# Graph attention with residual and layer norm: the left term worked out per four groups, context kept whole on chip, x loaded before the first strips

## The chip, the core and the metric

The kernel runs on one core of a Trainium2 chip. Its time is the device time of one execution in microseconds, given as the median of several runs. The engines are TensorE (PE; its weight loads are listed apart as PEld), VectorE (DVE), ScalarE (ACT), GpSimd (POOL) and SyncE (SP), which here issues every DMA.

## What is computed

N is 8192 rows, x is [8192, 256], context is [8192, 512], adj is an 8192 x 8192 matrix of zeros and ones in float32 (268 MB). Cut to what matters:

```python
in_fts = context @ W_common.T                 # 512 -> 256
left  = in_fts @ w_left + b_left              # one number per row
right = in_fts @ w_right + b_right            # one number per column
logits = left[:, None] + right[None, :]
logits = where(logits >= 0, logits, 0.2 * logits)
logits = where(adj <= 0, -inf, logits)
out = layernorm(x + relu(softmax(logits) @ x))
```

Neither term needs the 256-wide product: `context @ (W.T @ w)` is one dot product of 512 elements per row and side.

## The kernel before

**Layout.** The columns of adj are split into four quadrants of 2048 (`Q`, `NQ`), one per 32 partitions. A strip is 32 rows of adj (`B`), laid out as 128 partitions x 2048, 1 MB, and there are 256 of them (`NS`). Four strips make a group of 128 output rows (`SG`), and there are 64 groups (`NG`). The strips rotate through four buffers (`NB`); the transposed weights `T` have two halves, used by even and odd groups.

**Main part, per strip n.** SP loads it with four DMAs (`load_strip`, L172 to L176) once the buffer is free, that is after `transposed(n - 4)`. ACT turns it into a mask (`keep`, L351). DVE combines it with the column table `tab` (in PSUM) and the row's own word `arow[:, n]` (`masked`, L518, a maximum and a minimum), and transposes it in 32 x 32 blocks into `T` (`transposed`, L562). DVE's order is `masked(n + 1)`, `transposed(n)`; the first transpose of a group waits until PE has finished the group before last. Each float32 word holds a high and a low float16, and `X` holds x scaled, as a high and a low float16 too. PE makes a group's product from 64 x 3 matmuls: high with high (L291), low with high (L292), high with low (L295), each 128 x 257. Then follow the division, the residual, the mean, the variance and the normalisation, shared between DVE, ACT and POOL (L567, L332, L572, L336, L340, L255 to L259, L345), and a store.

**Setup.** SP loads W, two weight vectors and two biases, then the context in eight chunks of 2 MB (`NCH`, L200) through four places in `X`, then strips 0 and 1, then, after the left sums, strips 2 and 3, then x in four chunks (L212). Half of x (`xs1`) lies in `T[:, 1]`, the half of T that group 1 uses. DVE makes all 64 right dots and 24 of the left ones (`OWN`, L418), POOL multiplies for the 40 other left ones (L249), and ACT sums them (L305). Then one chain of small operations (L426 to L482) makes the exponentials, `tab` and all 256 columns of `arow`. ACT squares x in 64 steps to find its scale (L321), DVE makes the factors `Fx` (L489 to L504), ACT writes the 64 high parts of x (L326) and DVE the 64 low parts (L510). DVE has the first four strips transposed before the scale is known (they share no data with it), and it holds back `masked(4)` until the low parts are made. PE's group 0 waits for the high and low part of every block j in turn. SP issues nothing between the last x chunk and the end of the low parts (L214, L215); only then come two rows of x for the residual and strip 4:

```python
sp.wait_ge(s_xh, JB)
sp.wait_ge(s_xl, JB)
for g in range(2):
    load_xrow(g)
```

There is also a general path (`Else`) for data of a wide spread; it isn't taken with these inputs.

Of the kernel before, what the change touches and what calls it, by code (L numbers as in the profile page):

```python
# [11 lines left out]
AX = mybir.AxisListType  # L12

# [9 lines left out]
def build(nc, x, adj, ctx_in, w_common, w_left, b_left, w_right, b_right, out):  # L23
# [3 lines left out]
    P = 128  # L27
# [12 lines left out]
    NX = 4  # L40
    XC = JB // NX
    HB = JB // 2
    OWN = [j for j in range(JB) if j % 8 in (0, 3, 6)]
# [13 lines left out]
    with stack:  # L57
# [14 lines left out]
        LR = sb("LR", [P, 2, JB])  # L72
        E = sb("E", [P, 2, JB])
        Et = sb("Et", [P, 2, JB])
        word = sb("word", [P, 2, JB])
        gen = sb("gen", [P, 2, JB])
        F = sb("F", [P, JB])
        Fx = sb("Fx", [P, JB])
        SS = sb("SS", [P, JB])
        wcol = sb("wcol", [P, 2, HID // P])  # L80
        bias = sb("bias", [P, 2])
        small = sb("small", [P, 64])
        y = xs2[:, 0:NY, :]
        xrow = xs2[:, NY:NY + 2, :]

# [4 lines left out]
        word16 = word[:, :, :].rearrange("p c j -> p (c j)").bitcast(F16).rearrange("p (c j e) -> p c j e", c=2, e=2)  # L90
        cstage = [Xflat[:, s * CT * CIN:(s + 1) * CT * CIN].rearrange("p (t k) -> p t k", k=CIN) for s in range(4)]
        xs1 = T[:, 1, :, :].rearrange("p j m -> p (j m)").rearrange("p (j d) -> p j d", d=D)
        W = strip[:, 3, 0:2 * CIN].rearrange("p (h k) -> p h k", h=2)
        wrep = strip[:, 3, 2 * CIN:2 * CIN + 4 * P].rearrange("p (c h m) -> p c h m", c=2, h=2)
        vl = strip[:, 2, 0:CIN]
        prod = strip[:, 2, CIN:3 * CIN].rearrange("p (b k) -> p b k", b=2)

        def xrows(j):
            return xs1[:, j, :] if j < HB else xs2[:, j - HB, :]
# [10 lines left out]
        mxc, diag = small[0:3, 28:29], small[0:3, 29:32]  # L110

# [4 lines left out]
        pt = stack.enter_context(nc.psum_tensor("pt", [P, 512], F32))  # L116
        tab = stack.enter_context(nc.psum_tensor("tab", [P, NQ], F32))
# [5 lines left out]
        s_ctx = [sem(f"context_in{s}") for s in range(4)]  # L123
# [3 lines left out]
        s_vl = sem("v_left_copied")  # L127
        s_prod = sem("product_ready")
        s_sum = sem("product_summed")
        s_dot = sem("dots_done")  # L130
        s_lr = sem("left_right_ready")
# [14 lines left out]
        s_xl = sem("x_low_ready")  # L146
        s_one_col = sem("ones_column_steps")
# [23 lines left out]
        def _(sp):  # L171
# [14 lines left out]

            sp.dma_start(W, w_common.rearrange("(p h) k -> p h k", p=P)).then_inc(s_w, 16)
            for c, v in enumerate((w_right, w_left)):
                sp.dma_start(wcol[:, c, :], v.rearrange("(p h) -> p h", p=P)).then_inc(s_w, 16)
            for c, v in enumerate((b_right, b_left)):  # L190
                sp.dma_start(bias[:, c:c + 1], v.broadcast_to([P, 1])).then_inc(s_w, 16)
            for c in range(NCH):
                if c >= 4:
                    end = (c - 3) * CT
                    own = sum(j < end for j in OWN)
                    sp.wait_ge(s_dot, end + own)
                    sp.wait_ge(s_prod, end - own)
                for q in (0, 2, 1, 3):
                    rows = ctx_in[q * NQ + c * CT * B:q * NQ + (c + 1) * CT * B, :]
                    sp.dma_start(cstage[c % 4][q * B:(q + 1) * B, :, :],  # L200
                                 rows.rearrange("(t p) k -> p t k", p=B)).then_inc(s_ctx[c % 4], 16)
            for n in range(2):
                load_strip(n)
            sp.wait_ge(s_sum, JB - len(OWN))
            sp.wait_ge(s_v, 1)
            for n in range(2, NB):
                load_strip(n)
            for c in range(NX):
                dst = (xs1, xs2)[c // (NX // 2)][:, c % (NX // 2) * XC:(c % (NX // 2) + 1) * XC, :]
                for q in (0, 2, 1, 3):  # L210
                    r0 = q * NQ + c * XC * B
                    sp.dma_start(dst[q * B:(q + 1) * B, :, :],  # L212
                                 x[r0:r0 + XC * B, :].rearrange("(j p) d -> p j d", p=B)).then_inc(s_x[c], 16)
# [427 lines left out]
```

## Time and profile before

| | us |
|---|---|
| median of 3 runs | 1564.39 |
| lowest, highest | 1547.11, 1564.72 |
| profiled execution | 1557.17 |
| its span, first to last instruction | 1555.3 |

| engine | busy us | share |
|---|---|---|
| PE | 1379.9 | 89% |
| PEld | 1199.8 | 77% |
| DVE | 1269.4 | 82% |
| ACT | 685.9 | 44% |
| POOL | 110.2 | 7% |

The busy shares are means over a setup of about 200 us and a main part of about 1350 us, with different limits. For the setup the rows to read are those of single engines in order of time. For the main part they are one group's period and what ended the idle time before each line.

### The profile page before, as it was taken

What the parts mean: (1) busy time and instruction counts of PE and PEld (TensorE: products, weight loads), DVE (VectorE), ACT (ScalarE), POOL (GpSimd) and SP (SyncE); (2) the same over time, 40 slices, a digit from 0 to 9 for tenths busy, and PEclk for the clock granted to TensorE, in tenths of its full rate; (3) what the DMA queues carried; (4) which work ended last, traced back from release to release, by engine and by line L of the source; (5) the groups of instructions that cost most, each with busy time, mean ns of one, the idle gap of its engine ahead of it and who ended that gap; (6) DMA issues with size and microseconds to landing.
All of it is one profiled execution on the core that took longest, in us unless ns stands there. A gap on an engine that the chain in (4) does not pass through costs nothing.

```text
span 1555.3 us, 28279 instructions
## 1 busy us (share of the span) xinstructions
PE 1379.9 (89%) x12302; PEld 1199.8 (77%) x12302; DVE 1269.4 (82%) x1000; ACT 685.9 (44%) x852; POOL 110.2 (7%) x240
## 2 busy tenths in 40 slices
PE   1002379999999999999999999999999999999998
PEld 0002268888888888888888888888888888888887
DVE  4883698898888988888988888888889888889881
ACT  2458544444444444444444444444444444444440
POOL 4710000000000000000000000000000000000000
PEclk7555789999999999999999999999999999999999
DMA  9994598888888888888888888888888888888870
GB/s 212 270 200 87 139 220 208 221 206 207 211 208 216 213 205 211 206 207 224 203 210 210 208 210 220 205 207 211 209 218 211 205 212 208 207 223 204 208 177 12
DMA packets 85584, 312.82 MB, mean 201 GB/s; under 512 B 19792, under 2 KB 44368, under 8 KB 52688
## 3 DMA queue, kind: packets, MB, share of 16 engines
q1 hardware_dynamic: 85456, 310.98, 81.2%
q8 instruction: 96, 1.57, 0.5%
q14 instruction: 32, 0.26, 0.1%
HBM read 302.52 MB, written 8.39 MB: 200 GB/s over the span
## 4 chain that ended last, share of the span: by engine, by line
PE 87%; DMA 5%; SPq 4%; DVE 3%; ACT 1%; POOL 0%; issue 0%; POOLq 0%; DVEq 0%
PE ps L295 29%; PE ps L291 29%; PE ps L292 29%; DMA X<-in_L_gnn_context_dram 3%; SPq L212 2%; DVE X L510 2%; DMA xs<-in_x_dram 1%; SPq L200 1%; DMA strip<-in_adj_dram 1%; ACT pt L321 1%; SPq L175 1%; DVE gw L418 0%; DVE strip L518 0%; DVE T L562 0%; POOL strip L249 0%
## 5 line engine op out<-in xcount | busy, mean ns | idle before, releaser
L291 PE MATMUL ps<-X,T 128*128 128x257 f16 x4096 | 1117.3, 273 | 34.5 <-DVE T L562 32.8
L295 PE MATMUL ps<-X,T 128*128 128x257 f16 x4096 | 1125.2, 275 | 0.0
L292 PE MATMUL ps<-X,T 128*128 128x257 f16 x4096 | 1114.8, 272 | 0.0
L562 DVE STREAM_TRANSPOSE T<-strip 128x2048 f32<-128x2048 f32 x256 | 589.4, 2303 | 174.8 <-PE ps L295 174.8
L351 ACT ACTIVATE strip<-strip 128x2048 f32<-128x2048 f32 x256 | 488.8, 1910 | 413.7 <-DMA strip<-in_adj_dram 413.4
L518 DVE SCALAR_TENSOR_TENSOR strip<-tab,arow,strip 128x2048 f32<-128x2048 f32 x256 | 595.1, 2325 | 17.3 <-ACT strip L351 17.0
L291 PEld LDWEIGHTS ps<-X,T 128*128 128x128 f16 x4096 | 403.5, 99 | 85.0 <-DVE T L562 33.0
L292 PEld LDWEIGHTS ps<-X,T 128*128 128x128 f16 x4096 | 399.0, 97 | 61.3
L295 PEld LDWEIGHTS ps<-X,T 128*128 128x128 f16 x4096 | 397.2, 97 | 63.2 <-DVE X L510 7.5
L332 ACT ACTIVATE xs<-ps,small 128x256 f32<-128x256 f32 x64 | 30.4, 475 | 219.9 <-DVE small L567 219.9
L255 POOL TENSOR_SCALAR small<-small 128x1 f32<-128x1 f32 x64 | 12.3, 192 | 1398.9 <-ACT pt L340 1398.9
L336 ACT ACTIVATE small<-small 128x1 f32<-128x1 f32 x64 | 13.0, 203 | 156.2 <-DVE xs L572 156.2
L418 DVE SCALAR_TENSOR_TENSOR gw<-X,ps 128x512 f32<-128x512 f32 x88 | 54.2, 683 | 20.7 <-DMA X<-in_L_gnn_context_dram 20.7
L273 PE MATMUL pt<-ident,small 128*2 128x128 f32 x1 | 0.4, 372 | 69.0 <-DVE small L433 69.0
L273 PEld LDWEIGHTS pt<-ident,small 128*2 128x2 f32 x1 | 0.1, 80 | 70.1 <-issue 70.1
L249 POOL TENSOR_TENSOR strip<-X,strip 128x512 f32<-128x512 f32 x40 | 49.6, 1273 | 32.5 <-DMA X<-in_L_gnn_context_dram 32.5
L277 PE MATMUL pt<-ident,small 128*1 128x128 f32 x1 | 0.4, 372 | 55.5 <-DVE small L489 55.5
L277 PEld LDWEIGHTS pt<-ident,small 128*1 128x1 f32 x1 | 0.1, 79 | 55.6 <-DVE small L489 55.6
L305 ACT ACTIVATE strip<-strip 128x512 f32<-128x512 f32 x40 | 25.2, 630 | 38.8 <-POOL strip L249 38.8
L345 ACT ACTIVATE xs<-xs,small 128x256 f32<-128x256 f32 x64 | 37.5, 586 | 3.6 <-POOL small L259 3.6
L257 POOL TENSOR_TENSOR small<-small 128x1 f32<-128x1 f32 x64 | 35.2, 551 | 5.3
L340 ACT ACTIVATE pt<-xs,small 128x256 f32<-128x256 f32 x64 | 30.6, 478 | 2.1
(71 smaller groups left out, 198.3 us busy)
## 6 DMA issues: line engine op xcount, KB each, us to landing
strip<-in_adj_dram SPq DMA_DIRECT2D x1024, 256.0 KB, 4.6
X<-in_L_gnn_context_dram SPq DMA_DIRECT2D x32, 512.0 KB, 16.9
xs<-in_x_dram SPq DMA_DIRECT2D x64, 128.0 KB, 5.0
out_dram<-xs SPq DMA_DIRECT2D x64, 128.0 KB, 4.9
T<-in_x_dram SPq DMA_DIRECT2D x8, 512.0 KB, 13.9
xs<-in_x_dram SPq DMA_DIRECT2D x8, 512.0 KB, 14.1
strip<-in_L_gnn_W_common_dram SPq DMA_DIRECT2D x1, 512.0 KB, 3.6
wcol<-in_L_gnn_w_right_dram SPq DMA_DIRECT2D x1, 1.0 KB, 3.3
```

What stands on the lines that cost most here:

```text
L212: sp.dma_start(dst[q * B:(q + 1) * B, :, :], x[r0:r0 + XC * B, :].rearrange("(j p) d -> p j d", p=B)).then_inc(s_x[c], 16)
L249: nc.gpsimd.tensor_tensor(prod[:, m % 2, :], cstage[c % 4][:, t, :], vl, ALU.mult).then_inc(s_prod, 1)
L257: nc.gpsimd.tensor_tensor(st(5, o), st(4, o), power, ALU.pow).then_inc(s_rstd, 1)
L291: nc.tensor.matmul(ps[o][:, 0:D + 1], hi, X16[:, jb, 0:D + 1], start=(jb == 0), stop=False)
L292: nc.tensor.matmul(ps[o][:, 0:D + 1], lo, X16[:, jb, 0:D + 1], start=False, stop=False)
L295: m = nc.tensor.matmul(ps[o][:, 0:D + 1], hi, X16[:, jb, D + 2:2 * D + 3], start=False, stop=(jb == JB - 1))
L345: nc.scalar.activation(y[:, o, :], y[:, o, :], ACT.Identity, scale=st(5, o), bias=st(6, o)).then_inc(s_out, 1)
L351: nc.scalar.activation(s, s, ACT.Relu, scale=KEEP).then_inc(s_m, 1)
L418: nc.vector.scalar_tensor_tensor(out=gw[:, junk * CIN:(junk + 1) * CIN], in0=cstage[c % 4][:, t, :], scalar=1.0, in1=ps[side][:, 0:CIN], o ...
L510: nc.vector.scalar_tensor_tensor(out=X16[:, j, D + 2:2 * D + 2], in0=xrows(j), scalar=Fx[:, j:j + 1], in1=X16[:, j, 0:D], op0=ALU.mult, op ...
L518: nc.vector.scalar_tensor_tensor(out=s, in0=tab[:, :], scalar=arow[:, n:n + 1], in1=s, op0=ALU.max, op1=ALU.min).then_inc(s_p, 1)
L562: nc.vector.transpose(T[:, o, :, k * B:(k + 1) * B], strip[:, b, :].rearrange("p (j i) -> p j i", i=B)).then_inc(s_t, 1)
```

## The change

1. **The left term in blocks.** A block is four groups (`LB`), 16 strips (`LW`), and there are 16 blocks (`NLB`). The context rows of a block are loaded a second time, as 128 rows x 4 groups x 512 (1 MB, `load_left_rows`). DVE makes four dots of 512 elements (`left_dot`), spreads them over 16 columns (`left_by_strip`), PE brings them to all quadrants with one float32 matmul of 128 x 16 (`spread_left`), DVE, ACT and DVE again turn them into 16 columns of `arow`. Block 0 is made in the setup; block b is made during the four groups before it, at fixed steps of the strip count modulo 16: dots at 7 to 10, `left_by_strip` at 11, three small operations at 13, five at 14 (these wait for an ACT exponential issued behind `keep(16b)`), one wait at 15. PE's matmul stands behind the second group of each four. POOL's products, ACT's sums and DVE's 24 left dots of the setup go.
2. **Context whole on chip.** Eight places, in T and X, so no chunk waits for a dot. The dots' unused output goes to PSUM (`tab`) rather than to SBUF.
3. **x before the strips.** x follows the context; strips 0 to 3 follow x. The squares are taken two blocks at a time (32 steps), and they, and the factors, stand ahead of `keep(0)` and `masked(0)`. ACT then alternates one `keep` with ten high parts.
4. **Low parts shared.** POOL makes those of blocks 0 to 23 (`NPL`) in six batches of four, two operations each (scale in place, then subtract). DVE makes the 40 others. PE's group 0 makes all its 128 matmuls with the high part of x first and then the 64 with the low part, blocks 24 to 63 ahead of 0 to 23.
5. **Where SP waits.** Strips 4 to 7 are loaded as the buffers come free; the wait for the low parts stands behind strip 7, with left rows and the two residual rows behind it.
6. The unused output of the variance goes to SBUF rather than to PSUM. The biases are loaded behind the context.

```diff
 sp: (setup)
+            for c in range(2):
+                load_context(c)
+            load_left_rows(0)
+            for c in range(2, NCH):
+                load_context(c)
             ...
+            (x, with a wait for 16 dots ahead of its third chunk)
+            sp.wait_ge(s_v, 2)
+            for n in range(NB):
+                load_strip(n)
             for n in range(NS):
                 ...
                     sp.wait_ge(s_t, n + 1)
                     load_strip(n + NB)
+                if n == NB - 1:
+                    sp.wait_ge(s_xl, JB - NPL)
+                    sp.wait_ge(s_xp, NPL)
+                    load_left_rows(1)
+                    for h in range(2):
+                        load_xrow(h)
+                if n % LW == 12 and n // LW + 2 < NLB:
+                    b = n // LW + 2
+                    sp.wait_ge(s_ld, LB * b)
+                    load_left_rows(b)
 pool:
+            for j in range(0, NPL, XB):
+                rows = xrows(j, XB)
+                pool.wait_ge(s_xh, j + XB)
+                nc.gpsimd.tensor_tensor(rows, rows, Fx[...].broadcast_to([P, XB, D]), ALU.mult).then_inc(s_xf, 1)
+                pool.wait_ge(s_xf, j // XB + 1)
+                nc.gpsimd.tensor_tensor(X16[:, j:j + XB, D + 2:2 * D + 2], rows, X16[:, j:j + XB, 0:D],
+                                        ALU.subtract).then_inc(s_xp, XB)
 pe:
+            def spread_left(b):
+                pe.wait_ge(s_lm, b + 1)
+                if b >= 2:
+                    pe.wait_ge(s_la, 3 * (b - 1))
+                nc.tensor.matmul(pt[:, 0:LW], R[...], L[...], start=True, stop=True).then_inc(s_lb, 1)
                 m.then_inc(s_mm, 1)
+                if g % LB == 1 and g // LB + 1 < NLB:
+                    spread_left(g // LB + 1)
 act:
                 for n in range(NB):
                     keep(n)
-                square_sums()
-                high_parts()
+                    for j in range(n * 10, n * 10 + 10):
+                        high_part(j)
+                for j in range(NB * 10, JB):
+                    high_part(j)
                 ...
                     keep(n)
+                    if n % LW == 0:
+                        left_exponentials(n // LW)
 dve:
+                    if n % LW == LW - 1 and n + 1 < NS:
+                        left_step(n // LW + 1, n % LW)
                     if n + 1 < NS and n != SG - 1:
                         masked(n + 1)
                     transposed(n, n % NB, g, g % 2, k)
                     if n == SG - 1:
-                        x_factors()
                         low_parts()
-                        dve.wait_ge(s_xh, JB)
                         masked(n + 1)
+                    if n // LW + 1 < NLB and n % LW < LW - 1:
+                        left_step(n // LW + 1, n % LW)
```

## Rows read from the trace of the kernel before

**Rows 1.** Waits from 210 us on: who waited for whom, us, times, longest.
```profile
ACT strip L351 <- DMA strip<-in_adj_dram: 388.0, 186, 4.6
DVE T L562 <- PE ps L295: 174.8, 61, 3.0
DVE strip L518 <- ACT strip L351: 4.2, 9, 0.7
```

**Rows 2.** Timeline of DVE in a middle group: start, length, instruction, idle before, releaser.
```profile
482.57 2.31 DVE L562 STREAM_TRANSPOSE T<-strip 128x2048 f32<-128x2048 f32 x1 [2.96 <-PE ps L295]
...
503.90 2.31 DVE L562 STREAM_TRANSPOSE T<-strip 128x2048 f32<-128x2048 f32 x1 [2.96 <-PE ps L295]
```

**Rows 3.** Timeline of ACT in the same group.
```profile
491.27 1.92 ACT L351 ACTIVATE strip<-strip 128x2048 f32<-128x2048 f32 x1 [0.63 <-DMA strip<-in_adj_dram]
...
496.10 1.91 ACT L351 ACTIVATE strip<-strip 128x2048 f32<-128x2048 f32 x1 [2.42 <-DMA strip<-in_adj_dram]
```

**Rows 4.** Timeline of DVE in the setup: the last chunk's dots, the scale, group 1.
```profile
77.22 0.69 DVE L418 SCALAR_TENSOR_TENSOR gw<-X,ps 128x512 f32<-128x512 f32 x1 [1.24 <-DMA X<-in_L_gnn_context_dram]
...
77.84 0.68 DVE L418 SCALAR_TENSOR_TENSOR gw<-X,ps 128x512 f32<-128x512 f32 x1
...
141.80 0.22 DVE L489 TENSOR_REDUCE small<-SS 128x1 f32<-128x64 f32 x1 [27.66 <-ACT pt L321]
...
157.68 12.86 DVE L510 SCALAR_TENSOR_TENSOR X<-xs,Fx,X 128x256 f16<-128x256 f32 x32
181.05 2.35 DVE L518 SCALAR_TENSOR_TENSOR strip<-tab,arow,strip 128x2048 f32<-128x2048 f32 x1 [10.51 <-ACT strip L351]
...
199.15 2.31 DVE L518 SCALAR_TENSOR_TENSOR strip<-tab,arow,strip 128x2048 f32<-128x2048 f32 x1
201.38 2.30 DVE L562 STREAM_TRANSPOSE T<-strip 128x2048 f32<-128x2048 f32 x1
```

**Rows 5.** Timeline of ACT in the setup: squares at x's first, last chunk; high parts; strip 4.
```profile
104.72 0.39 ACT L321 ACTIVATE pt<-T 128x256 f32<-128x256 f32 x1 [7.58 <-DMA T<-in_x_dram]
...
133.16 0.39 ACT L321 ACTIVATE pt<-xs 128x256 f32<-128x256 f32 x1 [0.76 <-DMA xs<-in_x_dram]
...
144.35 12.89 ACT L326 ACTIVATE X<-T,Fx 128x256 f16<-128x256 f32 x32 [2.59 <-DVE Fx L504]
...
178.66 1.91 ACT L351 ACTIVATE strip<-strip 128x2048 f32<-128x2048 f32 x1 [8.64 <-DMA strip<-in_adj_dram]
```

**Rows 6.** Stretches: length, busy us (count) by engine, granted clock (1.00 = full), DMA share, GB/s.
```profile
30.00:35.00 5.00, 0.00 (x0) 0.00 (x0) 3.72 (x14) 2.41 (x8) 3.18 (x3) 0.50 1.07 234
80.00:85.00 5.00, 0.03 (x1) 0.06 (x1) 4.79 (x19) 2.69 (x8) 3.46 (x3) 0.50 0.13 43
175.00:180.00 5.00, 0.00 (x0) 0.00 (x0) 0.00 (x0) 1.34 (x1) 0.00 (x0) 0.57 1.01 234
400.00:600.00 200.00, 200.00 (x1802) 175.52 (x1801) 173.34 (x105) 88.24 (x87) 9.34 (x30) 1.00 0.85 211
```

**Rows 7.** Lines by form, first 180 us: busy us, mean ns, idle before.
```profile
L249 POOL TENSOR_TENSOR strip<-X,strip 128x512 f32<-128x512 f32 x40 | 49.6, 1273 | 32.5 <-DMA X<-in_L_gnn_context_dram 32.5
L305 ACT ACTIVATE strip<-strip 128x512 f32<-128x512 f32 x40 | 25.2, 630 | 38.8 <-POOL strip L249 38.8
L321 ACT ACTIVATE pt<-T 128x256 f32<-128x256 f32 x32 | 12.4, 388 | 9.5 <-DMA T<-in_x_dram 8.5
```

**Rows 8.** Timeline of PEld, float32 weight loads: a pair, and a pair alone.
```profile
9.22 0.50 PEld L267 LDWEIGHTS ps<-strip 128*128 128x128 f32 x2 [9.22 <-DMA bias<-in_L_gnn_b_left_dram]
...
142.81 0.49 PEld L279 LDWEIGHTS pt<-small,ones 1*128 1x128 f32 x2 [0.66 <-DVE small L491]
```

**Rows 9.** Chain that ended last: start, length, what; group 1's start and the end.
```profile
142.81 0.59 PE pt L279 x2
203.73 0.39 PE ps L291
1549.23 0.18 DVE small L567
```

More of the change, by code:

```diff
@@ L40, in build @@
     NX = 4
+    LB = 4
+    NLB = NG // LB
+    LW = LB * SG
+    NPL = 24
     XC = JB // NX
     HB = JB // 2
-    OWN = [j for j in range(JB) if j % 8 in (0, 3, 6)]
     WSCALE = 2.0 ** 10
@@ L310, in _ @@
             act.wait_ge(s_arg, 4)
             nc.scalar.activation(F[:, :], F[:, :], ACT.Exp).then_inc(s_exp, 1)
+            for j in range(HB):
+                if 2 * j % XC == 0:
+                    act.wait_ge(s_x[2 * j // XC], 64)
+                if j >= 1:
+                    act.wait_ge(s_ss, j)
+                nc.scalar.activation(ps[1][:, 0:2 * D], xrows(2 * j, 2).rearrange("p j d -> p (j d)"), ACT.Square,
+                                     accum_out=SS[:, j:j + 1]).then_inc(s_ss, 1)
@@ L324, in high_parts, with left_exponentials @@
                 act.wait_ge(s_Fx, 1)
[L325 to L326 removed]
+                nc.scalar.activation(X16[:, j, 0:D], xrows(j), ACT.Copy, scale=Fx[:, j:j + 1]).then_inc(s_xh, 1)
+            def left_exponentials(b):
+                act.wait_ge(s_la, b * 3)
+                nc.scalar.activation(E[:, lw], E[:, lw], ACT.Exp, scale=1.0 - SLOPE).then_inc(s_le, 1)
             def quotient(g, o, turn):
@@ L370, in general_steps @@
                         exponentials((it * NY + u) * SG + k, k % NB)
+                        if more and u * SG + k == 13:
+                            left_exponentials(it + 1)
             with act.If(general == 0):
@@ L388, in _ @@
             with act.Else():
-                square_sums()
-                high_parts()
+                for j in range(JB):
+                    high_part(j)
                 general_steps(0)
                 general_steps(1)
-                with act.Fori(2, NG // NY) as it:
+                with act.Fori(2, NG // NY - 1) as it:
                     general_steps(it)
+                general_steps(NG // NY - 1, more=False)
             for g in range(NG - 2, NG):
@@ L423, in _ @@
-            r, l = LR[:, 0, :], LR[:, 1, :]
+                    if j >= 4:
+                        dve.wait_ge(s_dot, j - 3)
+                    k = j % 4
+                    nc.vector.scalar_tensor_tensor(out=tab[:, k * CIN:(k + 1) * CIN], in0=cstage[c][:, t, :], scalar=1.0,
+                                                   in1=ps[0][:, 0:CIN], op0=ALU.mult, op1=ALU.mult,
+                                                   accum_out=r[:, j:j + 1]).then_inc(s_dot, 1)
+                if c == 2:
+                    dve.wait_ge(s_dot, (c + 1) * CT)
+                    dve.wait_ge(s_v, 2)
+                    dve.wait_ge(s_lc, 16)
+                    for q in range(LB):
+                        left_dot(0, q, lctx0, tab[:, q * CIN:(q + 1) * CIN])
+                    dve.wait_ge(s_const, 3)
+                    left_by_strip(0)
```

334 lines of the change are left out of this document (186 added, 148 removed).

## Prediction

> **What bounds the kernel now.** I read the stretches first, then the waits, then one group in order of time, then the setup engine by engine.
>
> In the main part PE is busy all the time, at the full clock, beside DMA engines at 0.85 and DVE at 173 of 200 us [rows 6]. A group's period is 503.90 - 482.57 = 21.33 us: DVE waits 2.96 us in each for PE [rows 2], 61 times in all [rows 1]. So neither the masks nor the loads set the pace. What could disturb it is how near the others are. ACT starts the mask of a group's first strip at 491.27, though its buffer was free when the transpose begun at 482.57 ended, at 484.80: 6.5 us pass from a free buffer to a landed strip, 8.4 to its mask [rows 2, 3]. DVE comes to the same strip 4 half-steps, about 9.1 us, after that transpose. The loads are thus nearly just in time, but DVE's 2.96 us lie behind them.
>
> The time that can be won is before group 1. PE starts group 1 at 203.73, and from there to the division of the last group 1345.5 us pass, 63 periods and 1.6 us [rows 9]. So the whole question is when group 1 starts, and whether 63 groups still take 1345.5 us. In front of 203.73 stand, going back: DVE's five masks and four transposes of group 1 from 181.05; strip 4, for which SP had waited until the low parts were done, so ACT got it at 178.66 only [rows 4, 5]; the 64 low parts up to 170.5; the scale of x, whose last square ended at 141.8; the last x chunk at 133.16; and the DMA stream before it, which had a hole at 80 to 85 us (0.13 busy, 43 GB/s) while SP waited for the left sums [rows 4 to 6].
>
> **The change part by part.** I rebuild the setup from the stream of DMAs.
>
> *Context.* The last chunk lands at 77.22 [rows 4]. The stream was never idle up to there (1.07 busy at 234 GB/s in one of its stretches, rows 6 show it), so "no chunk waits for a place" buys nothing, and POOL and ACT leaving the left dots buys nothing before 77.22 either. Block 0's left rows, 1.05 MB ahead of chunk 2, cost 1.05/0.234 = 4.4 us: 81.6.
>
> *The chain to `tab`.* DVE has 8 dots behind the last chunk, not 11, at 0.61 each: 86.6, against 84.0. The 16 copies into `arow` become one. All this, and the exponentials, now lie under x's transfer, since x is what is waited for: worth nothing.
>
> *x.* Chunks land (133.16 - 104.72)/3 = 9.5 us apart [rows 5]. Without the hole and the strips in front, four of them from 81.6 end at 119.6, against 133.16: 13.5 us won.
>
> *Squares.* Behind the last chunk come 8 steps of 512 rather than 16 of 256. A 256-wide step takes 0.54 us ((141.80 - 133.16)/16), of which the operation is 0.39; a 512-wide operation takes 0.63 [rows 5, 7]. So 0.75 to 0.78 a step, 6.1 us against 8.6. The scale chain stays at 144.35 - 141.80 = 2.6 us. High parts start at 119.6 + 6.1 + 2.6 = 128.3, 16 us earlier than 144.35.
>
> *What is late next.* The strips follow x: at 1.05 MB and 234 GB/s, 4.5 us each, they land at 124.1, 128.6, 133.1 and 137.6. `keep(0)` fits under the scale chain. Before, the first four masks and transposes lay in the time in which x was loaded; that cover is gone, and they now stand in the path. ACT alternates ten high parts (0.403 each, 12.89/32, [rows 5]) and a `keep` (1.85): `keep(3)` ends at 128.3 + 30 x 0.403 + 3 x 1.85 = 146.0. DVE, following it, makes `masked(3)` and the transposes of strips 2 and 3 (2.24 us each, from 199.15 to 201.38, [rows 4]): 146.0 + 6.7 = 152.7. Only then come DVE's 40 low parts at 0.402 (12.86/32): 16.1 us, 168.8. ACT's high parts end at 128.3 + 25.8 + 5.6 = 159.7, ahead of them. So the sharing with POOL saves 24 x 0.402 = 9.6 us, and the lost cover costs 24.4.
>
> *Group 1.* Strips 4 to 7 are asked for when buffers come free (138.7 to 152.7), so they are there; the 10.51 us that DVE sat idle before 181.05 are gone, and so are the 2.5 us by which 181.05 to 203.73 is longer than nine such operations. Five masks and four transposes, 9 x 2.24 = 20.2 us: group 1 starts at 189.0. `masked(8)` is the doubtful one. It starts at 184.5 and needs strip 8, free at 175.5: plus 8.4, 183.9. It just fits.
>
> *POOL.* A 512-wide product takes it 1273 ns [rows 7]; by length a 1024-wide one 2.5 us, twelve of them 30.6 us, from 130 to 161. Bounds: the start-up is not doubled too (28 us), or the float16 and broadcast operands cost double (61 us, until 191). I take the first, as L249 is the nearest row. Up to 169 it has cover in DVE's own low parts. PE's group 0 runs from 152.7: 192 x 0.111 + 1.6 = 23 us, to 175.7, so 13 us ahead of group 1; its new order costs nothing.
>
> *PE.* 15 `spread_left` in a stream that is never idle. No row shows a float32 matmul of 128 x 16 at the full clock. The nearest: a pair of float32 loads takes 0.50 us including the latency of the second, so they start some 0.2 apart, and both of a single product's take 0.49 [rows 8]; a whole float32 matmul alone takes 0.59 at half clock [rows 9]. Part hides under the matmul before. Lower bound 0.2, upper 0.75; I take 0.45, nearer the pair of loads: 15 x 0.45 = 6.8 us (3 to 11).
>
> *DVE in the main part.* Four dots of 0.61 to 0.69, ten small operations: 4 us in 85.3, at most 2.2 within one group, against 2.96 of idle in each. Each group can be late without PE noticing until 4 us are gone, as DVE transposes one group ahead. At step 14 DVE waits for an ACT operation behind `keep(16b)`; ACT ends that mask at 493.19 [rows 3], DVE gets there at 484.80 + 4 x 2.24 + about 0.9 (residual and step 13, an estimate) = 494.7. Behind that wait stand `masked(16b)` and the rest, so it would show at once. Cost: nothing.
>
> *SP.* Left rows (1.05 MB, 14 times) stand ahead of strip 16b + 1. They push it by 4.4 us in a queue that is 0.85 busy. Its mask then ends at about 502 on the scale of rows 3, DVE needs it at 500; the transposes behind it move by about 0.3 us, with 3.4 to spare before PE runs dry. The queue recovers in two to three strips. Nothing.
>
> *Variance output to SBUF, biases later.* Off the path.
>
> **Sum.** 189.0 + 1345.5 + 6.8 = 1541.3 for the last division; behind it 1555.3 - 1549.23 = 6.1 us as before: a span of 1547.4, and 1557.17 - 1555.3 = 1.9 around it: 1549.3. Against the profiled 1557.17 this is 8 us less. The median before is 7.2 us above that execution, and the lowest run 10 below. With half the median's distance added I predict 1553.
>
> **Rivals.**
> A. *POOL and DVE disturb each other in the low parts.* POOL's last 8 us of work fall on DVE's 16 us of low parts. In the setup before, DVE kept its 0.61 us pace and POOL its 1273 ns side by side, but DVE's second input was in PSUM there (L418); the low parts read both in SBUF. If POOL stood still until 168.8, it would end at 176 to 177, and left rows, residual rows and strip 8 would be issued then: `masked(8)` 5 us late, group 1 at 194, 1554 in all; with the median's half 1558. If DVE is slowed too, some 4 us more: 1562. The Trainium skill states this as a rule ("GPSIMD Engine Reference", the table at its head: the SBUF interfaces are shared with VectorE, with contention for instructions that have two SBUF inputs). No row here shows it.
> B. *The second load of context collides.* If the left rows, alone or with the store and residual rows, make strip 16b + 1 more than 3.4 us later than worked out, PE stops at every block. At a full 4.4 us for each of 14 loads that is 62 us: about 1615, slower. Against it: DMA at 0.85, and only 9 waits of DVE for a mask, 4.2 us in all [rows 1, 6]. For it: that mask ends 0.6 us ahead of its use (496.10 + 1.91 = 498.01 [rows 3], and 503.90 - 2.96 - 2.31 = 498.63 [rows 2]).
> C. *PE's matmul costs more,* 2 us each with its two waits and the loads behind it: 23 us more, 1576. Against it: semaphore waits at a group's start show no gap in 21.33 = 192 x 0.111.
> D. *The setup is won in full:* x lands sooner (its chunks slower than 240 GB/s context before), the strips find less in their way, or the left rows hide. 8 to 10 us less: 1543.
>
> **How the numbers follow.** Forecast 0.45, A 0.26, B 0.06, C 0.08, D 0.15. The range takes the forecast with its bounds (group 1 by 4 us either way, `spread_left` 4 us either way), A and D, and part of the 17 us between runs: 1540 to 1568. A measurement of this kernel can tell about 2%, 31 us, from no change. To be faster by that, 1533 is needed, which no case gives: 0.03. Slower by that is B alone, and a part of C's tail: 0.06. Within 2%: 0.91.
>
> **What would show it.** DMA without a hole until 137 us; the last x chunk at 120; high parts from 128; the last transpose of group 0 at 153; DVE's low parts 153 to 169, with no idle time before `masked(4)`; PE's first matmul of group 1 at 189 (before 203.7). From there to the last division 1352 us, with fifteen steps of under 0.75 us and no wait of PE for DVE. POOL done by 161 (forecast) or 176 (A). A PE idle time once per four groups would mean B. The forecast is wrong if group 1 starts outside 184 to 198, or if 63 groups take over 1360 us.

## The result, and the profile of the changed kernel

| | before | after |
|---|---|---|
| median, us (20 runs each) | 1563.2 | 1551.0 |
| lowest, highest | 1547.1, 1566.0 | 1547.0, 1555.0 |
| profiled execution | 1557.17 | 1551.78 |
| PE's first matmul of group 1 | 203.73 | 195.97 |
| last group's division | 1549.23 | 1543.87 |
| between the two | 1345.5 | 1347.9 |

The ratio of the times is 0.992 (95% interval 0.991 to 0.993): 12 us less, and within the 2% that the prediction calls no change. It lies inside the predicted range, 2 us below the predicted 1553.

The setup on DVE, in order of time (start, length, instruction, idle before, releaser), answers to [rows 4]. L491 is a dot of context, L564 the first step of x's scale, L625 `masked`, L669 `transposed`, L586 a low part, L674 the division.

```profile
75.75 0.69 DVE L491 SCALAR_TENSOR_TENSOR tab<-X,ps 128x512 f32<-128x512 f32 x1 [4.18 <-DMA X<-in_L_gnn_context_dram]
...
85.26 0.70 DVE L491 SCALAR_TENSOR_TENSOR tab<-X,ps 128x512 f32<-128x512 f32 x1 [4.21 <-DMA X<-in_L_gnn_context_dram]
...
131.14 0.19 DVE L564 TENSOR_REDUCE small<-SS 128x1 f32<-128x32 f32 x1 [31.86 <-ACT ps L367]
...
133.55 2.35 DVE L625 SCALAR_TENSOR_TENSOR strip<-tab,arow,strip 128x2048 f32<-128x2048 f32 x1
...
157.87 5.16 DVE L586 SCALAR_TENSOR_TENSOR X<-xs,Fx,X 128x256 f16<-128x256 f32 x8
162.95 12.75 DVE L586 SCALAR_TENSOR_TENSOR X<-T,Fx,X 128x256 f16<-128x256 f32 x32
175.73 4.61 DVE L625 SCALAR_TENSOR_TENSOR strip<-tab,arow,strip 128x2048 f32<-128x2048 f32 x2
...
193.61 2.30 DVE L669 STREAM_TRANSPOSE T<-strip 128x2048 f32<-128x2048 f32 x1
...
1543.87 0.17 DVE L674 RECIPROCAL small<-ps 128x1 f32<-128x1 f32 x1 [20.13 <-PE ps L342]
```

ACT, over the same time, answers to [rows 5]: the squares of x's last chunk (L367), the high parts (L374), and strip 8.

```profile
125.11 0.60 ACT L367 ACTIVATE ps<-T 128x512 f32<-128x512 f32 x1 [3.96 <-DMA T<-in_x_dram]
133.67 4.10 ACT L374 ACTIVATE X<-xs,Fx 128x256 f16<-128x256 f32 x10 [0.76 <-DVE Fx L580]
...
151.85 12.87 ACT L374 ACTIVATE X<-T,Fx 128x256 f16<-128x256 f32 x32
...
189.30 1.91 ACT L403 ACTIVATE strip<-strip 128x2048 f32<-128x2048 f32 x1 [17.37 <-DMA strip<-in_adj_dram]
```

The waits from 210 us on, with [rows 1], and a stretch of the main part, with [rows 6]:

```profile
ACT strip L403 <- DMA strip<-in_adj_dram: 470.4, 208, 7.4
DVE T L669 <- PE ps L342: 74.4, 46, 3.0
DVE strip L625 <- ACT strip L403: 44.4, 23, 3.5
```

```profile
400.00:600.00 200.00, 200.00 (x1804) 175.58 (x1802) 182.43 (x143) 87.89 (x87) 8.41 (x27) 1.00 0.90 224
```

PE is as busy as before. The left term's new work and the second load of context are to be seen all the same: DVE's busy time rises by 9 us in 200, DMA's share from 0.85 to 0.90, DVE's waits for a mask from 4.2 us to 44.4, and its waits for PE fall from 174.8 to 74.4. Of the 175 us that DVE used to wait for PE, some 60 have gone into its new work and 40 into waits for masks, but no wait of PE for DVE came of it: from the start of group 1 on, this trace has none.

### The profile page after: what moved, and what is told of

Read it like the earlier page. It is cut to its first block, busy times and chain, and to the rows that moved or that the text cites. A ratio compares the mean times of both kernels' runs of the same rounds, so it can differ in the third digit from the quotient of the medians.

```text
span 1550.0 us, 28426 instructions
## 1 busy us (share of the span) xinstructions
PE 1380.2 (89%) x12334; PEld 1206.2 (78%) x12334; DVE 1309.7 (85%) x1181; ACT 650.4 (42%) x722; POOL 84.7 (5%) x212
## 4 chain that ended last, share of the span: by engine, by line
PE 87%; SPq 7%; DVE 3%; ACT 2%; DMA 1%; issue 0%; POOL 0%; POOLq 0%; ACTq 0%; DVEq 0%
PE ps L342 29%; PE ps L339 29%; PE ps L340 29%; SPq L221 4%; SPq L239 3%; DVE X L586 1%; DMA T<-in_x_dram 1%; DVE strip L625 1%; ACT X L374 1%; DVE T L669 1%; ACT ps L367 0%; ACT strip L403 0%; SPq L233 0%; SPq L216 0%; PE pt L310 0%
## 5 line engine op out<-in xcount | busy, mean ns | idle before, releaser
L669 DVE STREAM_TRANSPOSE T<-strip 128x2048 f32<-128x2048 f32 x256 | 589.2, 2302 | 74.5 <-PE ps L342 74.4
L625 DVE SCALAR_TENSOR_TENSOR strip<-tab,arow,strip 128x2048 f32<-128x2048 f32 x256 | 597.7, 2335 | 51.3 <-ACT strip L403 50.6
L342 PEld LDWEIGHTS ps<-X,T 128*128 128x128 f16 x4032 | 390.9, 97 | 55.1
L491 DVE SCALAR_TENSOR_TENSOR tab<-T,ps 128x512 f32<-128x512 f32 x32 | 20.9, 726 | 22.6 <-DMA T<-in_L_gnn_context_dram 22.6
L474 DVE SCALAR_TENSOR_TENSOR xs<-xs,vl 128x512 f32<-128x512 f32 x60 | 38.9, 649 | 0.0
L310 PE MATMUL pt<-L,R 128*128 128x16 f32 x32 | 4.9, 230 | 34.2 <-DVE L L479 34.2
L491 DVE SCALAR_TENSOR_TENSOR tab<-X,ps 128x512 f32<-128x512 f32 x32 | 20.9, 725 | 16.7 <-DMA X<-in_L_gnn_context_dram 16.7
## 6 DMA issues: line engine op xcount, KB each, us to landing
X<-in_L_gnn_context_dram SPq DMA_DIRECT2D x16, 512.0 KB, 20.2
```

The source lines that it names most:

```text
L342: m = nc.tensor.matmul(ps[o][:, 0:D + 1], hi, X16[:, jb, D + 2:2 * D + 3], start=False, stop=(jb == JB - 1))
L474: nc.vector.scalar_tensor_tensor(out=junk, in0=rows[:, q, :], scalar=1.0, in1=vl[:, :], op0=ALU.mult, op1=ALU.mult, accum_out=l4[:, q:q + ...
L491: nc.vector.scalar_tensor_tensor(out=tab[:, k * CIN:(k + 1) * CIN], in0=cstage[c][:, t, :], scalar=1.0, in1=ps[0][:, 0:CIN], op0=ALU.mult, ...
L625: nc.vector.scalar_tensor_tensor(out=s, in0=tab[:, :], scalar=arow[:, n:n + 1], in1=s, op0=ALU.max, op1=ALU.min).then_inc(s_p, 1)
L669: nc.vector.transpose(T[:, o, :, k * B:(k + 1) * B], strip[:, b, :].rearrange("p (j i) -> p j i", i=B)).then_inc(s_t, 1)
```

## Experiments

Names that begin with `b_` are made from the kernel before, those with `a_` from the changed one. Times of a single profiled execution are compared inside the trace; medians are given where a kernel was run more than once (2 to 10 times). `before_again`, `a_no_reload`, `a_spread8`, `a_npl32`, `a_npl16` and `a_bias_first` were each run once.

### One edit of order on the kernel before

`b_early` moves only the place where SP waits for the low parts (point 5 of the change).

```diff
-            sp.wait_ge(s_xh, JB)
-            sp.wait_ge(s_xl, JB)
-            for g in range(2):
-                load_xrow(g)
             for n in range(NS):
                 ...
                     load_strip(n + NB)
+                if n == NB - 1:
+                    (the same waits and loads)
```

> The kernel before, with one edit: the two waits for the low parts (and the two residual rows behind them) stand behind strip 7 instead of ahead of strip 4. Theory 1 (the late strip 4 was the last wait before group 1, and nothing else of the change is needed to remove it): masked(4) follows the last low part at 170.5 us without a gap, five masks and four transposes take 20.2 us, group 1 starts at 190.8 instead of 203.7, and the time falls by 12 to 13 us, as much as by the whole change. Rival (the gain of the change needs x ahead of the strips and the low parts shared): group 1 moves by less than 5 us, since strips 4 to 7 or their masks find something else in their way.

Measured: 1552.5 us against 1563.8 for the kernel before, run beside it, ratio 0.992 (0.991 to 0.994). That is, within 1.5 us, the gain of the whole change. Its setup on DVE:

```profile
148.72 0.22 DVE L490 TENSOR_REDUCE small<-SS 128x1 f32<-128x64 f32 x1 [28.09 <-ACT pt L322]
...
151.88 12.79 DVE L511 SCALAR_TENSOR_TENSOR X<-T,Fx,X 128x256 f16<-128x256 f32 x32 [0.64 <-ACT X L327]
164.60 12.86 DVE L511 SCALAR_TENSOR_TENSOR X<-xs,Fx,X 128x256 f16<-128x256 f32 x32
179.22 4.61 DVE L519 SCALAR_TENSOR_TENSOR strip<-tab,arow,strip 128x2048 f32<-128x2048 f32 x2 [1.76 <-ACT strip L352]
```

The 10.51 us of idle time before strip 4's mask in [rows 4] have become 1.76; 64 low parts stand there as before. x's last chunk lands at 140.08 and group 1 starts at 199.45, not at the expected 190.8: the context came later in this execution than in the recorded one (its last chunk at 83.72, not 77.22). Set against the recorded trace group 1 moved by 4.3 us only, which taken by its words is the rival's case; but from x's last chunk to group 1 it is 59.4 us, where the recorded trace has 70.6, and the median fell by 11 us. That is Theory 1.

`b_early_x` also puts x's first two chunks ahead of SP's wait for the left sums, so that the hole of [rows 6] is filled.

```diff
             for n in range(2):
                 load_strip(n)
+            for c in range(2):
+                load_x(c)
             sp.wait_ge(s_sum, JB - len(OWN))
             sp.wait_ge(s_v, 1)
             for n in range(2, NB):
                 load_strip(n)
+            for c in range(2, NX):
+                load_x(c)
```

> b_early and, besides, x's first two chunks ahead of SP's wait for the left sums, which left the DMA engines nearly idle at 80 to 86 us. Theory 1 (everything up to group 1 hangs on the last x chunk): the last x chunk lands 5 to 6 us sooner (127.5 instead of 133.2), group 1 starts at 185, the time is 18 us below the kernel before. Rival (ACT's 64 squares or DVE's transposes of strips 2 and 3 become the bound): the x chunk lands sooner, but the high parts start less than 3 us sooner.

Measured: 1560.8 us, ratio 0.998 (0.996 to 0.999), so 8 us worse than `b_early`, where 18 us below the kernel before were expected. Filling the hole in this way was worth nothing; the rival came true, with ACT's squares as the bound. ACT's order is four `keep`, then the squares, and strip 2 now comes behind the two chunks:

```profile
115.94 1.91 ACT L357 ACTIVATE strip<-strip 128x2048 f32<-128x2048 f32 x1 [16.84 <-DMA strip<-in_adj_dram]
```

ACT stood 16.84 us in front of that strip, and could not turn to the x chunks loaded ahead of it; then 64 squares of 0.54 us in a row, without a wait for x, ended at 156.7, against 148.7.

### The kernel before, once more

> The kernel before, profiled once more. In the profile that the prediction rests on, the context chunks landed 9.1 to 7.6 us apart, the last at 77.2 us; in b_early, whose first 90 us are the same code, 9.4 us apart, the last at 83.7. Theory (the pace of the context varies from execution to execution, and the recorded one was a quick one): here the last chunk lands at 83 to 84, group 1 starts at about 210, and the time is about 1563. Rival (what follows the context, or that it is code of this kernel, sets the pace): 77 again, group 1 at 204, 1557.

```profile
74.21 0.69 DVE L418 SCALAR_TENSOR_TENSOR gw<-X,ps 128x512 f32<-128x512 f32 x1 [2.51 <-DMA X<-in_L_gnn_context_dram]
83.43 0.69 DVE L418 SCALAR_TENSOR_TENSOR gw<-X,ps 128x512 f32<-128x512 f32 x1 [2.44 <-DMA X<-in_L_gnn_context_dram]
...
186.36 2.35 DVE L518 SCALAR_TENSOR_TENSOR strip<-tab,arow,strip 128x2048 f32<-128x2048 f32 x1 [10.15 <-ACT strip L351]
```

Measured: 1561.6 us. The same program had its last context chunk at 83.43, not at 77.22 [rows 4], its last x chunk at 138.82, group 1 at 207.67 and the last division at 1553.69. So the execution that the prediction was built on had a context load 6 us faster than this one. Against this execution the changed kernel is 9.8 us shorter inside the trace (1553.69 - 1543.87), which is near the 12 us between the medians; against the recorded one it is 5.4 us.

With this execution the gain can be laid out from x's last chunk to group 1, each term the distance between two rows. A 0 for the masks of group 0 means that they lay under x's transfer:

| us | before again | after | `b_early` |
|---|---|---|---|
| x's last chunk lands | 138.8 | 125.1 | 140.1 |
| squares behind it | 8.6 | 6.0 | 8.6 |
| scale, factors | 3.2 | 2.4 | 3.2 |
| masks and transposes of group 0 | 0 | 24.3 | 0 |
| low parts on DVE | 25.6 | 17.9 | 25.6 |
| idle before strip 4's mask | 10.2 | 0 | 1.8 |
| five masks, four transposes | 21.3 | 20.2 | 20.2 |
| sum of the six | 68.9 | 70.9 | 59.4 |
| group 1 starts | 207.7 | 196.0 | 199.5 |

x first wins 14 to 15 us at the front; behind it POOL wins 7.7, the paired squares 2.6 and the shorter scale chain 0.8. 24.3 us go back because group 0's masks have lost the transfer of x as their cover. Together these terms come to about 1 us. What remains, 10.2 us of idle time and 1.1 of the masks, is about what the strip loads of point 5 bring alone.

### Is the left term free for DMA and DVE?

`a_no_reload` takes out the loads of left rows in the main part.

```diff
-                if n % LW == 12 and n // LW + 2 < NLB:
-                    b = n // LW + 2
-                    sp.wait_ge(s_ld, LB * b)
-                    load_left_rows(b)
...
-  dve.wait_ge(s_lc, (b + 1) * 16)
+  dve.wait_ge(s_lc, 32)
```

> The changed kernel without the 14 loads of left rows in the main part (blocks 2 to 15); DVE makes its dots from the rows of block 1, so the left term of rows from 1024 on is another. In the changed kernel DVE waited 50.6 us in all for masks, 44 of them in the main part, and PE never waited. Theory 1 (the left rows push the strip behind them, and the 3 us of idle time a group swallow it): DVE's waits for masks fall to below 10 us, its waits for PE grow by about as much, and the period and the time stay (within 1 us). Theory 2 (the loads cost PE something after all): from group 1 to the last division 1348.1 us becomes 1346 or less.

```profile
DVE T L665 <- PE ps L338: 118.1, 61, 3.0
DVE strip L621 <- ACT strip L399: 2.1, 6, 0.6
```

Measured: 1549.5 us. This kernel computes another left term from row 1024 on; the work of the engines is the same. From group 1 to the last division 1348.3 us pass, against 1347.9 with the loads, no difference: the seven traces that have the changed kernel's main part with each `spread_left` issued once, this one among them, lie between 1347.6 and 1348.8. The loads cause the late masks (44.4 us of DVE's waits fall to 2.1, and its waits for PE grow from 74.4 to 118.1), and PE never sees it. In the changed kernel one such place reads:

```profile
495.74 2.35 DVE L625 SCALAR_TENSOR_TENSOR strip<-tab,arow,strip 128x2048 f32<-128x2048 f32 x1 [2.57 <-ACT strip L403]
...
518.33 2.31 DVE L669 STREAM_TRANSPOSE T<-strip 128x2048 f32<-128x2048 f32 x1 [1.96 <-PE ps L342]
```

The mask came 2.57 us late, and still DVE had to wait 1.96 us for PE at the next group's first transpose.

### What does `spread_left` cost on PE?

`a_spread8` issues each of its matmuls eight times.

```diff
-  nc.tensor.matmul(pt[:, 0:LW], R[...], L[...], start=True, stop=True).then_inc(s_lb, 1)
+  for i in range(8):
+      m = nc.tensor.matmul(pt[:, 0:LW], R[...], L[...], start=True, stop=True)
+  m.then_inc(s_lb, 1)
```

> The changed kernel with every spread_left matmul issued eight times instead of once (the same result written eight times). From the start of group 1 to the last division the changed kernel took 1348.1 us, 2.6 us more than the kernel before, 0.17 us for each of 15. Theory 1 (a float32 matmul of 128 x 16 costs PE 0.17 us wherever it stands): 7 x 15 x 0.17 = 18 us more. Theory 2 (it costs 0.34 to 0.5 us, of which the matmuls around it hide most): 36 to 50 us more.

Measured: 1574.6 us. From group 1 to the last division: 1371.9 us, 24.0 more than 1347.9, for 15 x 7 = 105 matmuls: 0.23 us each, more than the 18 us of Theory 1 and less than the 36 of Theory 2. The 15 of the changed kernel cost 1347.9 - 1345.5 = 2.4 us together with their waits, 0.16 each; the six traces with the main part of the kernel before lie between 1345.5 and 1346.6, so 2.4 is known to about 1 us. One of the 15 can be seen in place in the changed kernel (L310), first PE and then the weight loads, with the same loads alone in the setup as the last row:

```profile
218.79 0.27 PE L342 MATMUL ps<-X,T 128*128 128x257 f16 x1
218.90 0.29 PE L310 MATMUL pt<-L,R 128*128 128x16 f32 x2
219.04 0.27 PE L339 MATMUL ps<-X,T 128*128 128x257 f16 x1
```

```profile
218.79 0.30 PEld L310 LDWEIGHTS pt<-L,R 128*128 128x128 f32 x2
46.35 0.50 PEld L310 LDWEIGHTS pt<-L,R 128*128 128x128 f32 x2 [35.35 <-issue]
```

In the stream, at a granted clock of 1.00, both loads take 0.30 us and begin with the matmul ahead, and the next matmul starts 0.14 us behind `spread_left`; alone in the setup, at 0.50, they take 0.50.

### Do POOL and DVE disturb each other?

`a_npl32` and `a_npl16` change how many low parts POOL makes.

```diff
-    NPL = 24
+    NPL = 32        (a_npl16: 16)
```

> The changed kernel with 32 low parts on POOL instead of 24. Theory 1 (where POOL works too, DVE's low parts take 0.64 us instead of 0.40, as the first ones did in the changed kernel, and POOL isn't slowed): POOL takes 8 batches of 4.13 us, from 135.5 to 168.6, so some 16 of DVE's 32 low parts take 0.64 and the other 16 take 0.40; they take 17 us together, and group 1 starts within 1.5 us of where it did (1 us sooner). Theory 2 (the slow first parts had another cause, such as the half of x they read): 8 fewer parts take 5 us off, since all of that half is POOL's now, and group 1 starts 5 us sooner.

> The changed kernel with 16 low parts on POOL instead of 24. POOL ends at about 152, before DVE's low parts begin. Theory 1 (DVE's first low parts were slow because POOL worked at the same time): all 48 take 0.40 us, 19.3 us together, 1.4 us more than the 17.9 of the changed kernel, and group 1 starts 1.4 us later. Theory 2 (another cause, such as the half of x they read): the 16 that read this half take 0.64 and the total is 23 us, group 1 5 us later.

With 32, DVE makes only 32 low parts, and they take 21.66 us, which neither theory of `a_npl32` had (17 us and less); with 16 it makes 48, in 19.05 us, as Theory 1 of `a_npl16` had it; with 24, 40 in 17.9. Both kernels took 1552.37 us. The reason is to be seen when the group of `a_npl32` is taken apart, DVE first, POOL below (L281 scales, L285 subtracts):

```profile
153.66 0.47 DVE L586 SCALAR_TENSOR_TENSOR X<-T,Fx,X 128x256 f16<-128x256 f32 x1
154.05 2.35 DVE L586 SCALAR_TENSOR_TENSOR X<-T,Fx,X 128x256 f16<-128x256 f32 x1
156.32 2.11 DVE L586 SCALAR_TENSOR_TENSOR X<-T,Fx,X 128x256 f16<-128x256 f32 x1
158.36 2.35 DVE L586 SCALAR_TENSOR_TENSOR X<-T,Fx,X 128x256 f16<-128x256 f32 x1
...
164.95 0.47 DVE L586 SCALAR_TENSOR_TENSOR X<-T,Fx,X 128x256 f16<-128x256 f32 x1
```

```profile
151.95 1.90 POOL L281 TENSOR_TENSOR xs<-xs,Fx 128x1024 f32<-128x1024 f32 x1
153.99 2.13 POOL L285 TENSOR_TENSOR X<-xs,X 128x1024 f16<-128x1024 f32 x1
156.08 2.08 POOL L281 TENSOR_TENSOR xs<-xs,Fx 128x1024 f32<-128x1024 f32 x1
158.30 2.13 POOL L285 TENSOR_TENSOR X<-xs,X 128x1024 f16<-128x1024 f32 x1
```

A low part takes 0.47 us alone. Beside POOL each takes about as long as POOL's instruction, 2.11 to 2.36 us, and ends up to 0.3 us behind it: one low part for each of POOL's instructions. POOL loses only the 0.18 us by which L281 grows. In these rows the two take turns by whole instructions rather than share a rate, and with long instructions on POOL and short ones on DVE nearly all of the loss is DVE's. The Trainium skill says it so ("SBUF — State Buffer", section on the two separate sides of SBUF): the port pair that VectorE and GpSimd share is locked for a whole instruction, and a VectorE instruction with two SBUF inputs needs it. The trace agrees. With 24, one low part, from 158.30 to 160.65, met POOL's last subtraction (158.24 to 160.37) and lost 1.9 us:

```profile
158.24 2.13 POOL L285 TENSOR_TENSOR X<-xs,X 128x1024 f16<-128x1024 f32 x1
158.30 2.35 DVE L586 SCALAR_TENSOR_TENSOR X<-xs,Fx,X 128x256 f16<-128x256 f32 x1
```

With 16 none did (POOL ends at 150.7), and the 8 more low parts cost 3.2. So 24 is the best of the three by DVE's rows, by about 1 us.

### The pace of the context load

The chunks of the changed kernel land 9.46 us apart, at 222 GB/s, where [rows 6] has 234. My first thought was that the two bias transfers, now behind the context, had left the 16 DMA engines in step with each other. `a_bias_first` puts them back ahead of it.

```diff
+            for c, v in enumerate((b_right, b_left)):
+                sp.dma_start(bias[:, c:c + 1], v.broadcast_to([P, 1])).then_inc(s_b, 16)
             for c in range(2):
                 load_context(c)
             load_left_rows(0)
```

> The changed kernel with the two bias loads ahead of the context, as in the kernel before. The prediction took the context at the pace of the kernel before (8.5 us a chunk, speeding up from 9.1 to 7.6), the changed kernel shows 9.46 throughout. Theory 1 (the small DMAs ahead put the DMA engines out of step with each other, and so on different quadrants): the chunks land 8.5 us apart and the last at about 78. Theory 2 (it is where the chunks are written, T before X, or that no chunk waits): 9.46 apart as in the changed kernel, the last at 85 to 88.

Measured: 1553.7 us. The chunks land 9.36 us apart, the last at 87.73: not the cause. The other thought was the order of the transfers: a chunk is four DMAs of 512 KB, each for the 32 partitions of one quadrant. `a_fine_context` makes sixteen of 128 KB of them, so that the quadrants alternate four times as often.

```diff
-                for q in (0, 2, 1, 3):
-                    rows = ctx_in[q * NQ + c * CT * B:q * NQ + (c + 1) * CT * B, :]
-                    sp.dma_start(cstage[c][q * B:(q + 1) * B, :, :], ...)
+                for h in range(4):
+                    for q in (0, 2, 1, 3):
+                        r0 = q * NQ + (c * CT + h * CT // 4) * B
+                        rows = ctx_in[r0:r0 + CT // 4 * B, :]
+                        sp.dma_start(cstage[c][q * B:(q + 1) * B, h * CT // 4:(h + 1) * CT // 4, :], ...)
     (dve)
-                dve.wait_ge(s_ctx[c], 64)
+                dve.wait_ge(s_ctx[c], 256)
```

> The changed kernel, with each context chunk loaded by 16 DMAs of 128 KB (two rows a partition, quadrants in turn) instead of 4 of 512 KB. In the changed kernel a 2 KB packet of the context takes 160 ns (median) and one of the left rows, whose DMA writes all 128 partitions, 94 ns. Theory (packets are slow where the DMA engines work on one quadrant of 32 partitions at a time, and quicker when they are on several): chunks land 7 to 8 us apart instead of 9.46, the last at about 70 instead of 85.3, and group 1 starts 10 us or more sooner. Rival (the rate comes from the source in memory or from the packet size): 9.4 us apart as before; SP's issues, 16 x 0.46 = 7.4 us a chunk, don't show.

Measured: 1538.1 us, ratio 0.983 (0.981 to 0.985); the last chunk lands at 69.79, group 1 starts at 179.72. Two stretches while context is loaded, the changed kernel and `a_fine_context` (columns as in [rows 6]):

```profile
60.00:65.00 5.00, 0.00 (x0) 0.00 (x0) 2.11 (x8) 0.00 (x0) 0.00 (x0) 0.50 1.06 222
```

```profile
60.00:65.00 5.00, 0.00 (x0) 0.00 (x0) 3.01 (x9) 0.00 (x0) 0.00 (x0) 0.50 1.06 282
```

The DMA engines show the same share, 1.06, with 222 and with 282 GB/s: a full share does not say that they move what they can. Two more stretches say the same. The one transfer of the setup that covers all 128 partitions at once, the left rows, makes the chunk behind it land 13.08 us after the one before (24.85 to 37.93), 3.6 us more than the 9.46 of the others; while it moves, the changed kernel reads 380 GB/s. And the recorded execution of the kernel before reached 306 with DMAs of 512 KB for one quadrant each, so the size of these DMAs alone does not set 222 (the changed kernel first, then the kernel before):

```profile
24.00:26.00 2.00, 0.00 (x0) 0.00 (x0) 1.15 (x3) 0.00 (x0) 0.00 (x0) 0.50 1.04 380
```

```profile
65.00:70.00 5.00, 0.00 (x0) 0.00 (x0) 4.21 (x15) 2.17 (x6) 3.62 (x4) 0.50 1.06 306
```

The Trainium skill ("SBUF — State Buffer", the section on the DMA port swizzle) has it that a transfer's rate depends on how many of 16 ports its partitions reach, and by its mapping one quadrant reaches half of them. That fits the slow chunks and the fast left rows. For the 282 and the 306, whose DMAs cover one quadrant each too, transfers to different quadrants would have to be under way together, and no run here shows that, nor the ports themselves. The edit also makes the DMAs smaller and alternates the quadrants at once, and no run separates the two. So the gain of the edit is shown, and its cause is argued.

`b_early_fine` makes the same edit on `b_early`.

> b_early with the context chunks in 16 DMAs of 128 KB instead of 4 of 512 KB, through the same four places. Theory (the finer order of quadrants is what counts, and the whole context on chip isn't needed for it): the last chunk lands at 70 to 72 us instead of 83.7, since 8 chunks 7.2 us apart still leave the 6.2 us that POOL and the 6.7 us that DVE need for one; everything up to group 1 moves by 12 us, about 1540. Rival (chunks 4 to 7 wait for the dots of chunks 0 to 3 and SP's queue runs dry): less than half of that.

Measured: 1540.1 us, ratio 0.985 (0.982 to 0.988); chunks 8.0 to 8.5 us apart, the last at 72.39; x's last chunk at 128.52, group 1 at 187.9, again 59.4 us later. So the edit is worth 12 to 13 us in either order, by two runs of each.

### The best of both orders

`a_best` adds to `a_fine_context` x in eight chunks (`NX = 8`) and six rather than ten high parts between the first masks. `b_best` adds only `NX = 8` to `b_early_fine`.

```diff
-    NX = 4
+    NX = 8
 a_best, act:
-                    for j in range(n * 10, n * 10 + 10):
+                    for j in range(n * 6, n * 6 + 6):
```

> The changed kernel with three edits: the context in 16 DMAs a chunk (as a_fine_context, 1538.1), x in eight chunks instead of four, and six high parts instead of ten between two of ACT's first masks. With a_fine_context x's last chunk landed at 108.9, 8 pairs of squares followed it, and group 1 started at 179.6. Expected from the profile: 4 pairs instead of 8 behind the last chunk, 3 us less; masks then follow the strips' landings (4.5 us apart) instead of the high parts, 3 us less; some 1 us back, as more of DVE's low parts now lie beside POOL's. Group 1 at 174 and 1532 to 1533. Rival (the strips, which land last of all, are the bound once the squares are short): group 1 at 177 or later, 1536.

> The kernel before with its three edits of order and size: the waits for the low parts behind strip 7, the context in DMAs of 128 KB (one 128 x 512 block per quadrant each), and now x in eight chunks instead of four. Theory (both orders of x and the first strips are equally good once their tails behind the last x chunk are equally short): behind the last x chunk stand 8 squares of 0.54 us rather than 16, so 4.3 us go from the tail of 59.4 us, group 1 starts 55 us after the last x chunk and, at the same pace of the context, at about 184 instead of 187.9; median about 1536, the same as the changed kernel with the same two sizes (1535.3). Rival (the squares of earlier chunks fill the time, ACT is the bound from the first chunk on): ACT is behind the DMAs already when the last chunk lands, the tail stays within 1 us of 59.4, and the median stays at 1540.

| | x's last chunk | group 1 | last division | median | ratio |
|---|---|---|---|---|---|
| `a_best` | 114.28 | 182.26 | 1529.86 | 1535.3 | 0.981 (0.978 to 0.984) |
| `b_best` | 125.46 | 180.53 | 1526.32 | 1534.0 | 0.981 (0.980 to 0.983) |

`b_best` did what was expected, 55.1 us from x's last chunk to group 1. `a_best` missed: group 1 was expected at 174. x's last chunk landed at 114.28, 5.4 us later than in `a_fine_context`, since its context came slower in this execution (last chunk at 76.14). From there to group 1 it takes 68.0 us rather than 70.8: the shorter way to the first mask wins 2.0 and the fewer high parts between the masks 4.3, but these also brought the first low part forward to 140.70, into POOL's work, and

```profile
140.70 8.62 DVE L588 SCALAR_TENSOR_TENSOR X<-xs,Fx,X 128x256 f16<-128x256 f32 x8
```

eight low parts took 8.62 us rather than 3.2, by the same lock, where `a_fine_context` had 5.12. Both beat both kernels of the case; between the two there is no difference that the runs can tell, and `b_best` needs neither the blocks of the left term nor POOL.

## Why the prediction came out right

The forecast case is the one that happened, within 2 us, and its mechanism is the right one: group 1 starts sooner, the masks of group 0 lose their cover, and the main part keeps its pace. But several of its terms were off and partly cancel, so that so small an error is partly luck.

- **Context, last chunk: 81.6 predicted, 85.3 measured.** The term was 77.22 + 4.4. The left rows moved the chunk behind them by 3.6, so that part was nearly right. The 77.22 was one execution's, and `before_again` shows 83.43: I took the pace of a single profile for the kernel's. The rows could not have shown the difference; the distance between the runs, 17 us, was the hint.
- **x, last chunk: 119.6 against 125.1.** 3.7 us of it from the context; the other 1.8 is that the four chunks of x took 39.9 us and not 38.0 (the last three landings are 10.5 and 9.9 us apart).
- **Squares and scale: 8.7 against 8.4** (125.11 to 133.55). Right, term by term.
- **High parts to the end of group 0's transposes: 24.4 against 24.3.** The step I was least used to, that the masks lose their cover and stand in the path, is right to 0.1 us. It is what made the large change small.
- **Low parts: 16.1 against 17.9.** Rival A's mechanism, with another victim: POOL did not stand still, DVE did, for 1.9 us.
- **POOL: 30.6 us predicted, 24.8 measured** (135.53 to 160.37). A 1024-wide operation took 1.89 or 2.14 us, so length is not the whole price: the 1273 ns at 512 [rows 7] hold a start-up. Had it taken 30.6, POOL would have ended at 166, and the lock would have cost DVE about 7 us rather than 1.9 (3.2 instructions of 2.55 us, of which all but 0.4 each is lost). That is worked out from the rows of `a_npl32`, not run.
- **Strip 8: "it just fits".** It did: DVE's mask of it starts at 191.38 with no idle time, and ACT's part of it ended at 191.21.
- **Group 1: 189.0 against 196.0,** inside the 184 to 198 that I named, by 5.5 us of x and 1.8 of the lock, less 0.3 of squares and scale.
- **`spread_left`: 6.8 us against 2.4,** below even the lower bound of 3. The step that failed is the 0.45 us, taken from weight loads that PE waited for ([rows 8]: 0.50 and 0.49, the first at a granted clock of 1.00, the second at 0.50). In the stream, at the full clock, the pair takes 0.30 and lies beside the matmul ahead: 0.14 us from `spread_left` to the next matmul, as the rows under `a_spread8` show.
- **The main part otherwise: nothing, and nothing it was** (B). Its warning sign, the late mask, came true: waits of DVE for a mask rose tenfold. The stop of PE did not, since each group has 2.96 us of idle time on DVE to take it up. `a_no_reload` confirms both. C fell with the 2.4 us, and with the 0.23 us for each further matmul in `a_spread8`. D's mechanisms, x sooner or the left rows hidden, did not come.
- **Half of the median's distance,** 3.6 us, was added for what the profile happened to be. The profiled sum of 1549.3 came out as 1551.8: +7.0 for group 1, -4.4 for `spread_left`. The slow context that the 3.6 us stood for was thus in the first term already; the changed kernel's median is 0.8 us below its profile, so 1553 came out 2 us high by errors of both signs, and that is luck as much as working.

What the prediction did not see: that point 5 alone would give the whole 12 us. All the numbers for it were there: without the wait for strip 4, 10.51 us of idle time and 2.5 of the masks behind it, with x unmoved.

## What to carry to other kernels

When a load is moved ahead of another, price the work that had been lying under it: here x came 14 us sooner, and 24 us of masks came out into the open. Before a large rearrangement, try its smallest edit by itself, above all the one that only moves a wait; one such move gave as much as six points together. And a setup that waits for DMA, as this one does, should be read in GB/s, not in busy share, and over more than one execution.

## What the runs showed of the hardware

- GpSimd and VectorE took turns by whole instructions when VectorE read both inputs from SBUF: a VectorE instruction of 0.47 us took 2.11 to 2.36 beside GpSimd's 1024-wide operations (`a_npl32`), and GpSimd's scaling grew from 1.90 to 2.08. A VectorE instruction with one input in PSUM was not held up: 0.69 us for a dot beside the products of [rows 7], and 2.35 for a mask beside POOL's low parts.
- Context in DMAs of 512 KB for one quadrant of 32 partitions each ran at 222 to 236 GB/s in most executions, and rose to 306 in the recorded one of the kernel before. In blocks of 128 KB that alternate quadrants it ran at 250 to 294 (four executions), and one DMA over all 128 partitions at 380. The share was 1.04 to 1.08 in the stretches shown and in nearly all others.
- The pace of one and the same context load differs between executions: the last chunk of the kernel before landed at 77.22 and at 83.43. What sets it is open; the place of the bias transfers does not.
- A float32 matmul of 128 x 16 with its own weights cost 0.16 to 0.23 us in a PE stream that never waited, at a granted clock of 1.00; its pair of loads took 0.30 us there, and 0.50 alone in the setup at 0.50.
